# Skip term summed in PSUM and copied out by ScalarE, with three edits in the last two stages of a fused layer

## What is computed

```python
h   = einsum('bct,bcd->bdt', x, w[subject]) + bias       # per-sequence mixing of positions
x, z = split(h @ in_proj.T); xc = silu(causal_conv4(x))  # 1024 channels
dt_r, B, C = split(xc @ x_proj.T)                        # 128, 16, 16
delta = softplus(dt_r @ dt_proj.T + bias)
state = state * exp(delta * A) + (delta * xc) * B        # 16 states a channel, a scan over positions
y   = (sum_n state[n] * C[n] + xc * D) * silu(z)         # xc * D is the skip term
x1  = x + y @ out_proj.T
x2  = x1 @ W.T + adapter of the sequence (rank 16)
out = x1 + shared_expert(x2) + sum of 4 of 16 routed experts(x2)
shared_expert: silu(x2 @ G.T) * (x2 @ U.T) @ D.T, inner width 704
routed expert: the same with inner width 352, chosen by a group-limited top-4 gate
```

## Time and profile before

| | us |
|---|---|
| median of 3 runs (1875.52 to 1881.6) | 1880.81 |
| profiled execution, its own time | 1879.41 |
| its span | 1877.6 |
| mean granted TensorE clock | 0.942 of full |
| busy in the span: PE / DVE / ACT / POOL | 1646.6 / 1457.8 / 818.9 / 1060.1 |

### The profile page before, as it was taken

One profiled execution on the slowest core, in us unless ns is written; L12 is line 12 of the kernel. 1 busy time (PEld: TensorE's weight loads), 2 busy tenths in 40 slices (PEclk: granted clock), 3 DMA queues, 4 the chain that ended last, 5 costly groups with the idle time before them and its releaser, 6 DMA issues. The chain is left out here.

```text
span 1877.6 us, 28500 instructions
## 1 busy us (share of the span) xinstructions
PE 1646.6 (88%) x7932; PEld 1211.5 (65%) x7932; DVE 1457.8 (78%) x1948; ACT 818.9 (44%) x1220; POOL 1060.1 (56%) x825
## 2 busy tenths in 40 slices
PE   8667868888998998878778999999979999999998
PEld 5255434554455554455445647778879999999997
DVE  3699999999999999999999826677346566565654
ACT  2656665566766667665664411000022233232322
POOL 0289579887599794898977470000044444344433
PEclk9869889999998999989988999999989999999999
DMA  5122112133322322222223342111155656665664
GB/s 128 38 59 68 57 41 76 60 93 81 79 96 85 90 90 68 91 90 62 74 73 112 113 165 70 67 68 44 61 138 127 175 130 172 164 135 141 155 175 70
DMA packets 129895, 182.20 MB, mean 97 GB/s; under 512 B 21379, under 2 KB 79491, under 8 KB 126660
## 3 DMA queue, kind: packets, MB, share of 16 engines
q1 hardware_dynamic: 109540, 131.85, 21.8%
q0 software_dynamic: 17760, 44.05, 12.0%
q10 hardware_dynamic: 2432, 4.33, 0.9%
HBM read 276.45 MB, written 37.36 MB: 167 GB/s over the span
## 5 line engine op out<-in xcount | busy, mean ns | idle before, releaser
L1194 POOL TENSOR_TENSOR arena_kept<-arena_kept,b_all 128x512 f32<-128x512 f32 x512 | 637.0, 1274 | 251.1 <-DVE arena_kept L1078 134.6
L1078 DVE TENSOR_TENSOR_SCAN arena_kept<-da,arena_kept 128x512 f32<-128x512 f32 x512 | 598.5, 1207 | 13.1 <-ACT da L927 8.1
L927 ACT ACTIVATE da<-arena_kept,a_neg 128x504 f32<-128x504 f32 x512 | 347.4, 684 | 244.6 <-DVE arena_kept L1078 238.6
L716 PE MATMUL hT<-ident_kept,arena_kept 128*128 128x128 f32 x2048 | 314.0, 300 | 145.1 <-DVE yacc L1090 88.6
L716 PEld LDWEIGHTS hT<-ident_kept,arena_kept 128*128 128x128 f32 x2048 | 256.4, 154 | 248.2 <-DVE arena_kept L1078 171.6
L1090 DVE SCALAR_TENSOR_TENSOR yacc<-hT,c_now,yacc 128x512 f32<-128x512 f32 x480 | 332.0, 735 | 4.4 <-PE hT L716 4.1
L2078 POOL DMA_INDIRECT out<-y,slots_kept x76 | 139.1, 1831 | 243.3 <-issue 174.4
L516 PE MATMUL bank<-hid,wt 128*128 128x512 f32 x512 | 239.9, 617 | 0.7 <-ACT hid L752 0.7
L516 PEld LDWEIGHTS bank<-hid,wt 128*128 128x128 f32 x512 | 98.8, 202 | 107.3 <-issue 105.7
L1946 ACT ACTIVATE gs<-egp 128x352 f32<-128x352 f32 x73 | 33.8, 464 | 237.5 <-PE eup L1278 236.9
L1714 POOL DMA_DIRECT2D slots_kept<-lists_kept x1 | 0.6, 554 | 222.7 <-DVE lists_kept L1664 222.7
(11 more groups left out here) (234 smaller groups left out, 3186.9 us busy)
## 6 DMA issues: line engine op xcount, KB each, us to landing
w_up_kept<-in_up_T SPq DMA_DIRECT2D x76, 1408.0 KB, 6.1
w_dn_kept<-in_dn_T SPq DMA_DIRECT2D x76, 768.0 KB, 7.4
b_all<-bt_scratch SPq DMA_DIRECT2D x128, 256.0 KB, 3.4
wt<-in_in_T SPq DMA_DIRECT2D x64, 256.0 KB, 3.0
wt<-in_out_T SPq DMA_DIRECT2D x32, 256.0 KB, 2.9
res<-in_x_pad SPq DMA_DIRECT2D x16, 256.0 KB, 3.6
x_scratch<-res SPq DMA_DIRECT2D x16, 256.0 KB, 2.1
wt<-in_w_T SPq DMA_DIRECT2D x16, 256.0 KB, 3.0
```

The costliest lines, as they stand in the source:

```text
L716: mm = nc.tensor.transpose(turned_in(j, m, t)[:, d * P:(d + 1) * P], h[:, m % RING, d, t * P:(t + 1) * P], ident[:])
L927: nc.scalar.activation(out[:, :, 1:], rows[:, :, 1:], ACT.Exp, scale=a_neg[:, d, n:n + 1]) \
L1078: nc.vector.tensor_tensor_scan(h[:, n % RING, i, :], da[i % RING][:], dbx[:, i, :], 0.0, ALU.mult, ALU.add).then_inc(scan_done, 1)
L1194: nc.gpsimd.tensor_tensor(dbx[:, i, :], u[:, d, :], b_all[:, m % RING, :], ALU.mult) \
```

## The change

Stage 1: `turn` puts an identity product of the `skip` tile in front of the four products that turn `yacc`, now plain matrix products into the same accumulation; ACT copies the bank to `skip` (`y_out`) in steps n = 0 and n = 1; `add_skip` is gone from DVE; the bank is counted as emptied by ACT.

```diff
-            by_act = name in EMPTIED_BY_ACT
+            by_act = name in EMPTIED_BY_ACT or name == "turn" and section == "body"
             def turn(at, half):
-                pe.wait_ge(sum_done, sums(at.block - 1, STEPS - 1, TB - 1) if half else sums(at.block, NST - 1, TB - 1))
+                of = at.block - 1 if half else at.block
+                pe.wait_ge(skip_ready, of * DT + (half + 1) * HT + SKIP0)
                 for d in range(HT):
                     bank = take(at, d)
+                    nc.tensor.matmul(bank[:], ident[:], skip[:, half * HT + d, :], start=True, stop=False)
+                    if d == 0:
+                        pe.wait_ge(sum_done, sums(of, half * NST + NST - 1, TB - 1))
                     for t in range(TB):
-                        mm = nc.tensor.transpose(bank[:, t * P:(t + 1) * P], yacc[:, t, d * P:(d + 1) * P], ident[:])
+                        mm = nc.tensor.matmul(bank[:, t * P:(t + 1) * P], yacc[:, t, d * P:(d + 1) * P], ident[:],
+                                              start=False, stop=(t == TB - 1))
...
+            def y_out(j, half, i):
+                at = Place("body", j, f"turn{half}")
+                act.wait_ge(bank_full, at.full + i + 1)
+                nc.scalar.copy(skip[:, half * HT + i, :], banks[at.uses[i].bank][:]).then_inc(act_emptied, 1)
...
                         decay(j, *divmod(m, NST), i)
-                        if m % NST == 1:
-                            first_state(j, m - 1, i)
+                        half = 1 - m // NST
+                        if runs(j, f"turn{half}"):
+                            if m % NST == 0 and i >= RING:
+                                y_out(j, half, i - RING)
+                            if m % NST == 1 and i < RING:
+                                y_out(j, half, i + RING)
+                        if m % NST == 1 and i:
+                            for t in range(0 if i == 1 else i, i + 1):
+                                first_state(j, m - 1, t)
...
-                nc.vector.tensor_tensor(skip[:, d, :], banks[at.uses[i].bank][:], skip[:, d, :], ALU.add).then_inc(dve_emptied, 1)
...
-                pool.wait_ge(dve_emptied, at.dve + i + 1)
+                pool.wait_ge(act_emptied, at.act + i + 1)
```

```diff
+BESIDE_UP = 3
+BESIDE_DOWN = (2, 7)
...
+                    groups = ((0, gp, g_full), (1, up, u_full))
+                    for half, bank, full in groups if f < KS - 1 else groups[:1]:
...
+                if j == 1:
+                    counts()
...
                 for t in range(TB):
-                    for _ in range(RANKS_BESIDE if j < 1 else 0):
-                        next(ranks, None)
                     dve.wait_ge(y_full, j * TB + t + 1)
                     nc.vector.tensor_tensor(res[:, t, :], yp[t % RING][:], res[:, t, :], ALU.add).then_inc(y_out, 1)
+                    for _ in range(BESIDE_DOWN[j] if j < 2 else 0):
+                        next(slot_steps if j else ranks, None)
```

```diff
-            sp.wait_ge(out_stored, 16 * NBLK)
...
+            sp.sem_inc(w_full[0], 32)
+            for r in range(RING):
+                sp.sem_inc(slots_full[r], 16)
             for r in range(TILES_AHEAD, LISTS):
                 load_slots(RUN_TILES + r - TILES_AHEAD, r)
...
-            first = run_parts(0)
+            first = 0, first_parts()
...
-            for s in range(YS - LAG, YS):
-                nc.vector.memset(y[:, s, :], 0.0).then_inc(y_zero, 1)
-            first = weight_parts(dve, 0)
+            first = first_parts()
...
+            for s in range(YS - LAG, YS):
+                nc.gpsimd.memset(y[:, s, :], 0.0).then_inc(y_zero, 1)
             pool.wait_ge(y_zero, LAG)
+            pool.wait_ge(keep["out_stored"], 16 * NBLK)
```

More of the change, by code:

```diff
@@ L1004, in c_out @@
                 nc.vector.tensor_copy(c_next[:], both[:, :, NST:]).then_inc(dve_emptied, 1)
-            def add_skip(at, half, i):
-                d = half * HT + i
-                dve.wait_ge(skip_ready, at.block * DT + (0 if half else d + 1) + SKIP0)
-                dve.wait_ge(bank_full, at.full + i + 1)
-                nc.vector.tensor_tensor(skip[:, d, :], banks[at.uses[i].bank][:], skip[:, d, :], ALU.add).then_inc(dve_emptied, 1)
             def gate_last(at, i):
@@ L1504, in sum_picks, with channels @@
                 mm.then_inc(picks_summed, 1)
+            def channels(part, k, half, f):
+                first = half * WHOLE + f * P if f < KS - 1 else 2 * WHOLE
+                return part[:, k, first:first + P]
             def expert(j):
@@ L1514, in expert @@
                         pe.wait_ge(x2_parts, j)
-                    for half, bank, full in ((0, gp, g_full), (1, up, u_full)):
-                        at_f = slice(half * SPAD + f * P, half * SPAD + (f + 1) * P)
+                    groups = ((0, gp, g_full), (1, up, u_full))
+                    for half, bank, full in groups if f < KS - 1 else groups[:1]:
                         for k in range(KM):
-                            mm = product(nc, bank[f % RING][:], [part[:, k, at_f] for part in (sup_hi, sup_lo)],
+                            mm = product(nc, bank[f % RING][:], [channels(part, k, half, f) for part in (sup_hi, sup_lo)],
                                          [x2_hi[:, k, :], x2_lo[:, k, :]], k == 0, k == KM - 1)
@@ L1612, in slots @@
-                step(nc.vector.tensor_tensor(more[:], upto[:, :, TILES - 1:TILES].broadcast_to([P, EXP, TILES]),
+                yield step(nc.vector.tensor_tensor(before[:], upto[:], before[:], ALU.subtract))
+                yield step(nc.vector.tensor_tensor(more[:], upto[:, :, TILES - 1:TILES].broadcast_to([P, EXP, TILES]),
                                              steps[:].unsqueeze(1).broadcast_to([P, EXP, TILES]), ALU.is_gt))
-                step(nc.vector.tensor_reduce(tiles[:], more[:], AX.X, ALU.add))
@@ L1615, in slots @@
-                step(nc.vector.tensor_tensor_scan(ends[:], ones[:, 0:EXP], tiles[:], 0.0, ALU.mult, ALU.add))
-                step(nc.vector.tensor_tensor(starts[:], ends[:], tiles[:], ALU.subtract))
-                step(nc.vector.tensor_tensor(place[:], within[:], before[:].rearrange("p e t -> p t e"), ALU.add))
-                step(nc.vector.scalar_tensor_tensor(out=place[:], in0=starts[:].unsqueeze(1).broadcast_to([P, TILES, EXP]),
+                yield step(nc.vector.tensor_reduce(tiles[:], more[:], AX.X, ALU.add))
@@ L1620, in slots @@
+                yield step(nc.vector.tensor_tensor_scan(ends[:], ones[:, 0:EXP], tiles[:], 0.0, ALU.mult, ALU.add))
+                yield step(nc.vector.tensor_tensor(starts[:], ends[:], tiles[:], ALU.subtract))
+                yield step(nc.vector.tensor_tensor(place[:], within[:], before[:].rearrange("p e t -> p t e"), ALU.add))
+                yield step(nc.vector.scalar_tensor_tensor(out=place[:], in0=starts[:].unsqueeze(1).broadcast_to([P, TILES, EXP]),
                                                     scalar=float(P), in1=place[:], op0=ALU.mult, op1=ALU.add))
-                step(nc.vector.scalar_tensor_tensor(out=place[:], in0=place[:], scalar=1.0, in1=sel[:],
+                yield step(nc.vector.scalar_tensor_tensor(out=place[:], in0=place[:], scalar=1.0, in1=sel[:],
@@ new lines, in slots @@
+                yield step(nc.vector.tensor_reduce(weight[:], match, AX.X, ALU.add))
+                yield step(nc.vector.tensor_scalar(slot_i[:], best[:, :, 0:TOP], -1.0, None, ALU.add))
+                yield step(nc.vector.tensor_scalar(part_i[:], slot_i[:], P - 1, None, ALU.bitwise_and))
+                yield step(nc.vector.tensor_copy(in_tile[:], part_i[:]))
+                yield step(nc.vector.tensor_scalar(part_i[:], slot_i[:], P.bit_length() - 1, None, ALU.logical_shift_right))
+                yield step(nc.vector.tensor_copy(of_tile[:], part_i[:]))
@@ L1698, in _ @@
                 next(ranks)
+            slot_steps = slots()
             expert(0)
             expert(1)
-            for _ in ranks:
-                pass
-            slots()
             for j in range(2, NBLK):
```

126 lines of the change are left out of this document (64 added, 62 removed).

## The result

The change made the kernel faster: 1866.21 us median of 5 runs (1862.84 to 1867.64) against 1879.82 of the kernel before (1875.52 to 1881.6), ratio 0.9929, 95% interval 0.9913 to 0.9946. On another chip, the same change once more: 1862.79, ratio 0.9908 (0.9893 to 0.9924). So the gain is 13.6 us in the first comparison and 18.2 in the second. The forecast was a gain of 26.7 and a time of 1853; the range of 1842 to 1867 held the first result by less than a microsecond.

A forecast was written before the change was run, and what follows sets the result against it. It took DVE's scans to bound stage 1 and PE the shared stage and experts. Gains of 1.5 (stage 1), 18.3 (shared stage) and 6.9 (experts' start) made 26.7 us, so 1853; range 1842 to 1867, its own 1847 to 1858.

The forecast's parts named there:

- the start of the experts: Way into the experts: barrier 3.8 us earlier, first low part of weights ready 3.1 us earlier; 6.9 us gained, bounds 3.8 and 8.
- (a): Shared stage: f = 5 loses 12 products in each of 4 blocks, 10.9 us gained; whole stage 18.3, bounds 15 to 21.
- the stage-1 sum: Stage 1, all seven turns: gains of 1.7 and 2.8 us less a loss of 3, so 1.5 us gained.
- the forecast's 2.1: Shared stage, block 0: PE's stall behind DVE's add and the low clock after it shrink but stay; 2.1 us gained.
- 5.6 + 5.4 - 0.3: Shared stage, blocks 2 and 3: block 2's stall and low clock go (5.6 us), fewer f = 5 products, less 0.3 for later picks.
- the tail: Shared stage and start of the experts together, forecast at 18.3 and 6.9 us gained, with bounds given as 22 to 29.
- turn1: Stage 1, second-half turns of blocks 1 to 3: ACT's copies fit its pauses; 0.9 us gained each, 2.8 in all.
- turn0: Stage 1, first-half turns of blocks 0 to 2: DVE's adds go but ACT is late next; 0.6 us gained each, 1.7 in all.
- Turn0 of block 3: Stage 1, block 3's first-half turn: ACT's copies delay decays with nothing to hide them; 3 us lost, 0.65 at full clock.
- Rival 1: Stage 1: PE's low clock at the turns delays banks and copies; 12.6 us lost, time 1866; chance 0.18.
- The sum of 3.8 for the stage: Stage 1 alternative: plain products count as PE activity, so the clock stays up and block 3's first-half turn loses nearer 0.65; 3.8 gained.
- a sign of being wrong in stage 1: Stage 1: forecast wrong if the stretch from 60 to 1075 us shrinks by over 6 us or grows.

The follow-up runs named there:

- full rows: The whole change, but the f = 5 down products of the shared stage contract all 128 rows again, the added 64 zeroed once by POOL; ratio 0.9899.
- the tail alone: Kernel before with only the edits of the shared stage, experts' start and raw-weight loads, stage 1 as before; 1859.01 us, ratio 0.9893.
- Two mixtures: The change with 128-row f = 5 products: new turns only in first halves of blocks 0 to 2 (1853.27 us), or everywhere except block 3's first half (1853.76 us).
- both pure forms: The change with 128-row f = 5 down products, with stage 1 as in the kernel before (1857.99 us, ratio 0.9880) or with all turns new (ratio 0.9899).

## Why the prediction was right or wrong

The sign of the whole and the order of the gains were right, and the size was wrong by half. Between the spans 12.2 us were gained instead of 26.7. The 14.5 that are missing: 6.8 in the shared stage, 2.8 in the scans, 1.8 at the barrier, 2.9 in the experts and 0.5 before the first scan, less 0.3 that the start of the experts gave beyond its forecast. The step of the prediction that failed is (a) of the shared stage, with its bounds of 15 to 21; smaller parts are the stage-1 sum, and the barrier and the experts, which it put at nothing.

*Shared stage, 18.3 forecast, 11.5 in the trace.* In the trace with full rows the stage shrinks by 18.2 (231.4 to 213.2), the forecast to a tenth; the six traces with full rows give 17.1 to 18.3, since block 0 scatters by 1.2, so the tenth is luck and the size is not. Block 0: 4.8 in that trace, the forecast's 2.1 and 12 products of 0.227. Block 1: 2.5 against 2.7. Blocks 2 and 3: 11.0 against 5.6 + 5.4 - 0.3 = 10.7 (one of the eight groups of picks, 16 products, moved from the one to the other). What failed is a term that step (a) did not have: it counted the gate and up products that go and took the down products, 72 instructions as before, for unchanged. They have another shape, and a change of shape was an operation that the trace of before did not show; it had no bound either. It measured 0.2 us a switch, 1.6 us a block, 4.6 us where nothing covers it; in the first trace of the change block 0 lost another 2 us, which the repeated change (218.1 for the stage) did not. The range had a slip of its own: the tail is given as 22 to 29, but the lower bounds of its two steps add up to 15 + 3.8 = 18.8, and 18.7 was measured.

*Stage 1, 1.5 forecast (-2 to 5).* In the seven traces that hold the whole stage-1 edit the scans take 988.9 to 993.0 us, mean 991.2, against 991.7, 991.9 and 992.5 with the old turns: 0.8 gained, less than the traces differ among themselves, and within the bounds of the step. By the parts: turn1 0.7 for 0.9, turn0 0.8 for 0.6, both near. Turn0 of block 3: forecast 3 at low clock and 0.65 at full clock, measured 2.0 to 2.6 and 0.6 to 0.7 by step 19. But most of the larger loss came back before the block ended, 0.3 to 0.7 staying; the step took a delay inside the block for one at its end. What is missing is the low clock. The step asked only whether it would stand in the turn; it went out of the turn, and came back behind it, where the output products have no slack. Rival 1 had the clock as mechanism and the place wrong; that its 1866 is the first median is luck. The 1.12 us of an old bank, set against 1.75 at full clock, were themselves taken at a clock of 0.50 (458.7 to 459.9 us of the trace before), so the new form adds more to PE at equal clock than the text says. On the turns' clock the Trainium skill, TensorE: Matmul & The Clock Gate, Part 4, was quoted against the row. The new turns of second halves stood at 1.00 in all 30 blocks, as its rule would have it; but each bank also got an identity product, and no run separates the form from the amount. The sum of 3.8 for the stage that was worked out by it did not come, for the low clock came behind the turn.

*Barrier, 0 forecast, 1.8 lost.* No step of the sum had it. It goes with a packet of PE's instructions among the last stores, in 14 traces without exception, and moving the packet out by PE's program alone took it away twice. The forecast could not have placed the packet from the rows it read.

*Start of the experts, 6.9 forecast, 7.2 in the trace,* 6.9 with the tail alone. POOL's zeroing, for which there was no row, took 1.45 us, and POOL then stood 3.4 us more for a load of slots, so it was covered.

*The experts, 0 forecast, 2.9 more.* They took 504.7 to 511.4 us in 14 traces in which nothing of their loop differed, 505.7 in the repeated change. It is scatter as far as these runs show; its cause, and that of the 511.4, stays open. The forecast compared one execution with one execution and left no room for it.

Signs: the scans of the first trace grew by 1.3 us, which the forecast had named as a sign of being wrong in stage 1 (those of the repeated change shrank by 0.1). First states at 13.4 and 15.5 us for 13.2 and 18, copies 0.58 us, banks 1.75 us apart, one group for f = 5, 2.5 us of PE's wait in block 0 for 3, none in block 2, 3.8 us for 4.3 at the experts: all but the 15.5 near. The sign that would have told of the miss, the length of the down products, was not on the list.

## What to carry to other kernels

Where an edit changes the shape of instructions that it leaves in place, cost them anew; zeroed rows that keep the shape can be cheaper than the rows they save, and shapes that must differ should stand side by side. Moving work from a busy engine to one that stands in front of it in the chain (here ACT, whose decays DVE waits for) was worth 0.7 to 0.8 of 2.35 us a turn here, and less than nothing in one; try it place by place. Two mixtures (1853.3 and 1853.8, ratios 0.9854 and 0.9851, 27 us under before) came out ahead of both pure forms (0.9880 with old turns, 0.9899 with new ones), though against the old turns the intervals touch. And when an edit keeps PE busier in one place, look for where its low clock goes next before booking the gain.

## What was not expected of the hardware

- A change between 128 and 64 rows of contraction costs PE 0.2 us each way (two loads 0.65 us apart in place of 0.45); the 64-row product itself takes as long as one of 128 (0.39 us).
- One 16384-byte packet of instructions among the last stores before a barrier made them land 1.78 us later; 124 instructions more, spread over PE's program far ahead of it, moved it out, and the added products of the turns had moved it in.
- PE's low clock moved with PE's work alone: in the turns of second halves in 12 of 12 blocks with the old form, in 0 of 30 with the new one, but behind it in 18 of the 30.
- Waits on a semaphore already reached may not be free: in the one trace with 48 instructions of them in front of PE's program, PE's first product came at 11.7 us, elsewhere at 7.3 to 8.2. The 124 that stood where PE had time to spare show no such cost.
